# Embedding moved out of its own stage into the first layer, and a third up slice in front of the projection

## Chip, cores and metric

One core of a Trainium2 chip runs the whole program. The metric is device time in microseconds; the median of the runs before is 5509.81 us (three runs, 5508.85 to 5511.06).

## The reference

32 sequences of 256 tokens, hidden width 192, 12 heads of 16. The part that the change touches:

```python
h = layer_norm(emb_word[input_ids] + emb_pos[:S][None], emb_ln_s, emb_ln_b)
for l in range(L):                       # L = 4, banded attention (+-64 tokens)
    a = band_attention(heads(h@Wq+bq), heads(h@Wk+bk), heads(h@Wv+bv), mask)
    h = layer_norm(h + a @ Wo[l] + bo[l], ln1_s[l], ln1_b[l])
    f = gelu(h @ W1[l] + b1[l])          # exact GELU, 4 x 192 columns
    h = layer_norm(h + f @ W2[l] + b2[l], ln2_s[l], ln2_b[l])
```

Behind it come `h + attn(layernorm(h))`, causal with rotary positions, and `h + moe(layernorm(h))`, 16 experts that choose their tokens, with a shared expert.

## The kernel before

`build` calls three stages, each in blocks of its own: `embed`, `tower` and `route`.

**embed** (lines 210 to 352) works on tiles of 128 tokens x 192. SyncE loads ids, positions, norm weights and the mask. VectorE cleans the ids (L295 to L299) and widens the mask by a maximum over 129 neighbours (L301 to L314); SyncE stores that mask to `am_d`. GpSimd gathers rows of the word table with one indirect transfer per tile (L273), 64 in all, and takes the root's power (L281). VectorE adds positions (L323), takes moments (L325, L328, L330) and normalises (L336, L343), four tiles at a time; SyncE writes them to `hbuf` in HBM (L258), which holds the hidden state of every layer.

**tower** starts with constants (loads from L1288, the columns of the mask from `am_d` at L1295) and `setup_dve`, whose casts and fills end in the semaphore `c_ok` (9), on which TensorE and GpSimd wait. Then `token_layers` runs the four layers, and a causal layer follows in the next block. Sequences go in pairs, one in slot 0 and one in slot 1. A **half-turn** works on five sequences at once, one per role, and every engine has its own in-order list for it (`tensor_token`, `scalar_token`, `vector_token`, `pool_token`, and `half` on SyncE):
- G: transpose the hidden state, project to queries and keys, split them into bf16 parts in `stack`.
- V: values; SyncE transposes the stack into `qkT` (L1324); the row maxima (L982) stand at the end of VectorE's list.
- F: first scores, whose row maxima are subtracted later.
- K: second scores, exponentials, products, the sums and the division on VectorE (L1008 to L1020), attention transposed (L453, ScalarE's copy `hT` in L776), projection (L580), residual and norm (L1050 to L916), transposed again (L589).
- B: the MLP of the sequence before: up (`pe_up`, L618 and L621), GELU (L815), down (`pe_down`, L632), residual sum (L1071) and norm.

Layer 1 begins with four half-turns in which only G, then G and V, and so on have work. Each layer is a loop of 14 pairs of half-turns and four written out. `pe_up` makes its six slices of 128 columns in two steps: `UP_BEGIN` in front of the projection, `UP_REST` behind it:

```python
            if K:
                pe_att_T(ph, pe, K)
            if B:
                pe_up(ph, pe, B, G, F, UP_BEGIN)
            if K:
                pe_project(ph, pe, K)
            if B:
                pe_up(ph, pe, B, G, F, UP_REST)
```

SyncE's half-turn issues, in this order: residual (F), transposes (V), hidden state of the next pair (G), maxima's transpose and copy (F), masks (F), a weight load, store (B). It waits in order for each.

Of the kernel before, what the change touches and what calls it, by code (L numbers as in the profile page):

```python
# [65 lines left out]
SCORE_LINKS = 1  # L66


NPAIR = 3
UP_BEGIN = (0, 1)  # L70
UP_REST = (2, 3, 4, 5)
# [119 lines left out]
def build(nc, a, out, B, L, V):  # L191
    ctx = ExitStack()
    with ctx:
# [10 lines left out]
        embed(nc, a, hbuf, am_d, B, V, (L + 1) * N)  # L204
        tower(nc, a, hbuf, am_d, xs, sd, out, B, L)
# [4 lines left out]
def embed(nc, a, hbuf, am_d, B, V, HROWS):  # L210

    N = B * S
    NT = N // P
    G = 4
    STEPS = NT // G
    PAST = 2
    MASK_LINKS = 15
    with ExitStack() as ctx:
        sb = lambda name, shape, dt: ctx.enter_context(nc.sbuf_tensor("emb_" + name, shape, dt))
        sem = Semaphores(nc)  # L220
        ids_raw = sb("ids_raw", [P, NT], I32)
        idf = sb("idf", [P, NT], F32)
        neg = sb("neg", [P, NT], F32)
        ids = sb("ids", [P, NT], I32)
        emb = sb("emb", [P, NT, D], F32)
        pos = sb("pos", [P, T, D], F32)
        lnw = sb("lnw", [P, 2 * D], F32)
        st = [sb(f"st{u}", [P, G, 6], F32) for u in range(2)]
        mv = [sb(f"mv{u}", [P, G, 2], F32) for u in range(2)]
        ve = [sb(f"ve{u}", [P, G], F32) for u in range(2)]  # L230
        half = sb("half", [P, G], F32)
        rstd = [sb(f"rstd{u}", [P, G], F32) for u in range(2)]
        z = [sb(f"z{u}", [P, G, D], F32) for u in range(2)]
        mi = sb("mi", [B, S], I32)
        PADW = S + 2 * W
        mw = [sb("mw0", [B, PADW], F32), sb("mw1", [B, PADW], F32)]
        in_sem, row_sem, mask_sem, am_st = sem("e_in"), sem("e_row"), sem("e_mask"), sem("e_amst")
        ids_ok, gathered = sem("e_ids"), [sem(f"e_gath{g}") for g in range(STEPS)]
        chain, var_ok, rstd_ok, z_ok, z_out, const_ok = (sem("e_chain"), sem("e_var"), sem("e_rstd"), sem("e_z"),
                                                         [sem(f"e_zout{u}") for u in range(2)], sem("e_const"))  # L240
        ctx.callback(sem.close)
        block = ctx.enter_context(nc.Block())

        @block.sync
        def _(sp):
            sp.dma_start(ids_raw[:], a["x"].rearrange("b (t p) -> p (b t)", p=P), allow_slow_non_contiguous=True).then_inc(in_sem, 16)
            sp.dma_start(pos[:], a["emb_pos"].rearrange("(t p) d -> p t d", p=P)).then_inc(row_sem, 16)
            sp.dma_start(lnw[:], a["emb_ln"].to_broadcast([P, 2 * D])).then_inc(row_sem, 16)
            sp.dma_start(mi[:], a["mask"]).then_inc(mask_sem, 16)

            sp.wait_ge(chain, MASK_LINKS)
            for c, f0, w in BAND_COLS:
                sp.dma_start(am_d[0:B, c:c + w], mw[0][:, f0:f0 + w]).then_inc(am_st, 16)
                sp.dma_start(am_d[B:B + NST, c:c + w], mw[0][0:NST, f0:f0 + w]).then_inc(am_st, 16)
            for g in range(STEPS):
                sp.wait_ge(z_ok, g + 1)
                rows = hbuf[g * G * P:(g + 1) * G * P, :]
                sp.dma_start(rows.rearrange("(t p) d -> p t d", p=P), z[g % 2][:]).then_inc(z_out[g % 2], 16)  # L258
                if g == 0:
                    rows = hbuf[HROWS:HROWS + G * P, :]  # L260
# [23 lines left out]
        def _(dve):  # L284
# [63 lines left out]
            for g in range(STEPS):  # L348
                if g + 1 < STEPS:
                    moments(g + 1)  # L350
# [1677 lines left out]
```

## Time and profile before

| | |
|---|---|
| median of the runs | 5509.81 us |
| the profiled execution | 5544.22 us, span 5542.4 us |
| TensorE busy | 5064.9 us (91%), 41842 matmuls |
| VectorE busy | 3498.0 us (63%) |
| ScalarE busy | 2573.6 us (46%) |
| GpSimd busy | 1152.9 us (21%) |
| mean granted TensorE clock | 0.978 of full |

A row of the instructions in time gives the start in us from the span's start, the time it took (merged with its like if there is a count xN), engine, source line, operation, what it writes and reads, and in brackets the idle time of the engine before it with what ended it. PEld is TensorE's weight load, SPq a transfer's issue on SyncE's queue. The table by stretches gives, for a stretch and its length, busy us and count of TensorE, its weight loads, VectorE, ScalarE and GpSimd, then the granted clock, the DMA engines' share and GB/s. "issue" is idle time for which the profile shows no releaser. Matmuls are pipelined; their starts say more than their ends.

### The profile page before, as it was taken

How to read it: one execution, taken by the hardware profiler on the slowest of the kernel's cores; microseconds unless marked ns; L12 is line 12 of the kernel's file. 1: busy time of each engine (PE TensorE's matmuls, PEld its weight loads, DVE VectorE, ACT ScalarE, POOL GpSimd, SP SyncE). 2: the span in 40 equal slices, each digit the busy share in tenths (PEclk: the TensorE clock that was granted, in tenths of full speed). 3: DMA queues.
4: the chain of work that ended last, by engine and by line, in shares of the span. 5: the costliest groups of instructions: out<-in, count | busy, mean ns of one | idle time of the engine just before them, and what ended most of it. 6: DMA issues, size and time to landing. Idle time of an engine off the chain costs nothing. (4 is left out here: it accounts for less than half of the span.)

```text
span 5542.4 us, 119208 instructions
## 1 busy us (share of the span) xinstructions
PE 5064.9 (91%) x41842; PEld 3972.4 (72%) x41842; DVE 3498.0 (63%) x8963; ACT 2573.6 (46%) x5128; POOL 1152.9 (21%) x1048
## 2 busy tenths in 40 slices
PE   0799999999999999999999999969999954999999
PEld 0577777777777777777777777747777742777766
DVE  6566666666666666666666666567777745333332
ACT  0355555555555555555555555535555630111111
POOL 6111111111111111111111111100000001545453
PEclk9999999999999999999999999989999976999999
DMA  6544444444444444444544444344444420333232
GB/s 106 105 88 92 97 92 89 107 93 98 91 88 90 103 101 95 89 88 94 105 101 88 90 97 94 67 93 96 92 101 95 95 69 17 65 83 81 67 87 41
DMA packets 1283995, 488.94 MB, mean 88 GB/s; under 512 B 1086659, under 2 KB 1270560, under 8 KB 1283872
## 3 DMA queue, kind: packets, MB, share of 16 engines
q1 hardware_dynamic: 1256224, 450.63, 37.3%
q0 software_dynamic: 27648, 36.72, 4.3%
q8 instruction: 71, 1.16, 0.1%
q14 instruction: 52, 0.43, 0.0%
HBM read 162.82 MB, written 60.28 MB: 40 GB/s over the span
## 5 line engine op out<-in xcount | busy, mean ns | idle before, releaser
L764 ACT ACTIVATE pT<-banks 128x384 f32<-128x384 f32 x1920 | 924.9, 491 | 768.8 <-PE banks L533 758.1
L982 DVE TENSOR_REDUCE mx<-banks 128x4 f32<-128x768 f32 x768 | 719.4, 950 | 294.3 <-PE banks L514 294.3
L1165 POOL TENSOR_TENSOR rstd<-ve,half 128x2 f32<-128x2 f32 x288 | 218.8, 760 | 3062.4 <-DVE ve L891 3062.4
L496 PE MATMUL banks<-maskb,eyeb 128*128 128x384 bf16 (+1 forms) x2304 | 719.0, 312 | 91.6 <-DVE mx L986 27.0
L514 PE MATMUL banks<-qkT 128*128 128x192 bf16 (+2 forms) x3840 | 633.5, 247 | 0.0
L533 PE MATMUL banks<-qkT 128*128 128x192 bf16 (+2 forms) x3840 | 630.8, 247 | 0.0
L632 PE MATMUL banks<-w,pT 128*128 128x192 f32 x3072 | 554.5, 330 | 0.0
L632 PEld LDWEIGHTS banks<-w,pT 128*128 128x128 f32 x3072 | 492.7, 190 | 42.4 <-issue 21.9
L496 PE MATMUL banks<-mseq,eyeb 128*128 128x384 bf16 x1536 | 501.9, 327 | 9.1 <-issue 4.4
L618 PE MATMUL banks<-nT,w 128*128 128x256 f32 x1920 | 472.5, 382 | 6.6 <-DMA b<-in_b 3.1
L1910 PE MATMUL ps_g<-exp_xT,exp_wg 64*128 64x512 f32 x1152 | 466.8, 600 | 10.8 <-issue 5.4
L1910 PE MATMUL ps_u<-exp_xT,exp_wu 64*128 64x512 f32 x1152 | 456.8, 592 | 4.8 <-DMA emb_emb<-in_emb_word,emb_ids 4.6
L533 PEld LDWEIGHTS banks<-qkT 128*128 128x128 bf16 x3840 | 376.8, 98 | 114.9 <-issue 0.9
L514 PEld LDWEIGHTS banks<-qkT 128*128 128x128 bf16 x3840 | 377.9, 98 | 106.9 <-issue 2.4
L474 PE MATMUL banks<-wqk,hTa 97*128 97x384 f32 (+1 forms) x1280 | 448.7, 492 | 4.3 <-ACT hTa L772 2.7
L815 ACT ACTIVATE pT<-banks,b 128x256 f32<-128x256 f32 x768 | 294.4, 483 | 336.7 <-PE banks L621 336.7
L554 PE MATMUL banks<-pT,vaug 128*32 128x192 f32 (+3 forms) x10752 | 413.5, 284 | 2.5 <-ACT pT L764 1.3
L1690 ACT ACTIVATE exp_sg<-ps_g 128x512 f32<-128x512 f32 x192 | 114.6, 597 | 643.9 <-PE ps_g L1910 558.9
L795 ACT ACT_TABLE_LOAD x320 | 410.6, 1283 | 5.7
L1807 DVE TENSOR_TENSOR exp_hid<-exp_sg,ps_u 128x512 f32<-128x512 f32 x192 | 132.1, 688 | 424.1 <-PE ps_u L1910 361.5
L618 PEld LDWEIGHTS banks<-nT,w 128*128 128x128 f32 x1920 | 347.3, 191 | 42.0 <-DMA b<-in_b 3.6
L554 PEld LDWEIGHTS banks<-pT,vaug 128*32 128x32 f32 x10752 | 284.5, 109 | 121.4 <-ACT pT L764 48.0
(202 smaller groups left out, 8745.1 us busy)
## 6 DMA issues: line engine op xcount, KB each, us to landing
hcur<-hbuf SPq DMA_DIRECT2D x164, 192.0 KB
resid<-hbuf SPq DMA_DIRECT2D x160, 192.0 KB, 2.5
amb<-am_d SPq DMA_DIRECT2D x130, 192.0 KB, 3.0
hbuf<-hout SPq DMA_DIRECT2D x128, 192.0 KB, 2.0
exp_wg<-in_ewg SPq DMA_DIRECT2D x16, 768.0 KB
exp_wu<-in_ewu SPq DMA_DIRECT2D x16, 768.0 KB
exp_wd<-in_ewd SPq DMA_DIRECT2D x16, 576.0 KB
xs<-xr SPq DMA_DIRECT2D x32, 272.0 KB, 2.2
```

The lines of the kernel that those rows point to most:

```text
L474: last = nc.tensor.matmul(bank[s][1 + t][:, 0:2 * D], hTa[s][rows_of(c), c, t * P:(t + 1) * P], wqk[rows_of(c), c, :], start=(c == 0), sto ...
L496: nc.tensor.matmul(part(dst), eyeb[:], part(mask), start=True, stop=ph is not tok)
L514: last = nc.tensor.matmul(dst[:, c0:c0 + w], qT[s][:, h, t * P:(t + 1) * P], kT[s][:, h, f0:f0 + w], start=False, stop=(t == T - 1), skip_ ...
L533: last = nc.tensor.matmul(dst[:, c0:c0 + w], kT[s][:, h, t * P:(t + 1) * P], qT[s][:, h, f0:f0 + w], start=False, stop=(t == T - 1), skip_ ...
L554: last = nc.tensor.matmul(dst[32 * j:32 * j + 32, at + f0:at + f0 + w], vaug[s][:, t, 4 * g + j, :], pT[s][:, (4 * g + j) % NPT, c0:c0 + w ...
L618: nc.tensor.matmul(up_bank(s, f), w1[:, f % 2, up_cols(ph, f)], nT[s][:, f % 2, :], start=True, stop=False)
L632: last = nc.tensor.matmul(bank[1 - s][0][:, t * D:(t + 1) * D], flat_pT(s)[:, f * S + t * P:f * S + (t + 1) * P], w2[:, f, :], start=(f == ...
L764: ph.inc(nc.scalar.activation(pT[s][:, h % NPT, :], bank[s][h % 2][:, 0:SCOLS], ACT.Exp, scale=SCALE), "p", s)
L795: ph.inc(nc.scalar.activation(spare[B.s][:, k:k + 1], zero[:], func), "tb", B.s)
L815: ph.inc(nc.scalar.activation(flat_pT(s)[:, f * S:(f + 1) * S], up_bank(s, f), ACT.Gelu, bias=b1[:, f:f + 1]), "g", s)
L982: last = nc.vector.tensor_reduce(mx[s][:, :, at].rearrange("p t h -> p h t"), src[:, :, 0:SCOLS].rearrange("p h (t k) -> p h t k", t=T), A ...
L1910: last = nc.tensor.matmul(dst[k % 2][:], w[u][rows, c, f * P:(f + 1) * P], xT[rows, c, n0:n0 + HALF], start=start, stop=stop)
```

## The change

`embed` goes, with its block and its end. `tower` loads ids, mask, positions and norm weights first; `first_dve` cleans the ids and widens the mask as before and makes the fills that were in `setup_dve`. GpSimd gathers the first two pairs. VectorE embeds sequences (0, 0) and (1, 0) straight into `hcur` (the numbers are slot and pair), runs the rest of `setup_dve`, then embeds (0, 1) and (1, 1) into two buffers `ring`. SyncE writes all four to `hbuf`. The other 28 are embedded one per half-turn in the first layer, two pairs ahead (argument `X`): GpSimd takes the root and later gathers the next sequence, once the ring buffer's old content has landed in `hbuf`; VectorE takes the moments at the head of its list and normalises in front of the projection's sum; SyncE stores the rows behind the mask load. Without a K (the first three half-turns) VectorE does both parts behind the stack. `load_hidden` waits until the rows are in `hbuf`. The first layer is a loop of its own on GpSimd, VectorE and SyncE. `UP_BEGIN` has three slices instead of two, in all layers and in the causal one.

```diff
+EMBED_AHEAD = 2
-UP_BEGIN = (0, 1)
-UP_REST = (2, 3, 4, 5)
+UP_BEGIN = (0, 1, 2)
+UP_REST = (3, 4, 5)
...
+        def embed_moments(dve, X):
+            s, x, ch = X.s, embed_rows(X), Chain(em, dve, X, "el")
+            dve.wait_ge(*((first_in[s], 16 * T) if x is hcur[s] else (gathered[s], X.it * (16 * T))))
+            ch.inc(nc.vector.tensor_tensor(x[:], x[:], pos[:], ALU.add))
+            ch.wait()
+            for t in range(T):
+                last = nc.vector.bn_stats(est[s][:, t, :], x[:, t, :])
+            ch.inc(last)
+            ch.wait_apart(row_in, 32)
+            for t in range(T):
+                last = nc.vector.bn_aggr(emv[s][:, t, :], est[s][:, t, :])
+            ch.inc(last)
+            ch.wait()
+            em.inc(nc.vector.tensor_scalar(eve[s][:], emv[s][:, :, 1], 1e-12, None, ALU.add), "var", s)
+            return ch
+
+        def embed_normalise(dve, X, ch):
+            s, x = X.s, embed_rows(X)
+            for t in range(T):
+                last = nc.vector.scalar_tensor_tensor(x[:, t, :], x[:, t, :], emv[s][:, t, 0:1], lnw[:, 0:D],
+                                                      ALU.subtract, ALU.mult)
+            ch.inc(last)
+            em.wait(dve, "rstd", s, X.it)
+            ch.wait()
+            for t in range(T):
+                last = nc.vector.scalar_tensor_tensor(x[:, t, :], x[:, t, :], erstd[s][:, t:t + 1], lnw[:, D:2 * D],
+                                                      ALU.mult, ALU.add)
...
+        def vector_token(ph, dve, G, V, F, K, B, X=None):
+            if X and K:
+                ec = embed_moments(dve, X)
             if K:
                 s = K.s
                 bc = Chain(ph, dve, K, "bl")
...
             if G:
                 dve_rest(ph, dve, G)
+            if X and K:
+                embed_normalise(dve, X, ec)
             if K:
                 ph.wait(dve, "wo_ps", s, K.it)
...
                 dve_stack(ph, dve, G, bass.ds(G.pair * (NST * T) + G.s * T, T))
+            if X and not K:
+                embed_normalise(dve, X, embed_moments(dve, X))
...
+        def pool_gather(pool, X):
+            s = X.s
+            early = isinstance(X.it, int) and X.it < EMBED_AHEAD
+            at = ids[:, X.it * (NST * T) + s * T:(X.it + 1) * (NST * T)] if early else now[s]
+            if not early:
+                pool.wait_ge(z_out[s], X.it * 16 + 16)
+                nc.gpsimd.tensor_copy(now[s][:], ids[:, bass.ds(X.it * (NST * T) + s * T, T)]).then_inc(now_ok[s], 1)
+                wait_apart(pool, now_ok[s], X.it - 1, ids_ok, 1)
+            for t in range(T):
+                pool.indirect_dma_start(embed_rows(X)[:, t, :], None, a["emb_word"],
+                                        bass.IndirectOffsetOnAxis(ap=at[:, t:t + 1], axis=0)
+                                        ).then_inc((first_in if embed_rows(X) is hcur[s] else gathered)[s], 16)
...
+        def pool_token(ph, pool, G, V, F, K, B, X=None):
             if F:
                 pool_masks(ph, pool, F)
+            if X:
+                pool_embed_rstd(pool, X)
             if K:
...
+            if X:
+                pool_gather(pool, embed_turn(1 - X.s, X.it + X.s))
             if B:
                 pool_rstd(ph, pool, B, "var2", "rstd2")
...
+                def store_rows(X):
+                    s = X.s
+                    wait_apart(sp, z_ok[s], X.it, c_in, 112)
+                    rows = hbuf[bass.ds(X.it * (NST * S) + s * S, S), :]
+                    sp.dma_start(rows.rearrange("(t p) d -> p t d", p=P), ring[s][:]).then_inc(z_out[s], 16)
+                def load_hidden(G, embedded):
                     tok.wait_apart(sp, "hT_ps", G.s, G.it, None, c_in, 112)
+                    if embedded:
+                        wait_apart(sp, z_out[G.s], G.it * 16 + 48, c_in, 112)
                     load_h(G.it + 1, G.s)
...
                     if F:
                         sp_maxima(tok, sp, F, c_in, 112)
                         load_masks(F)
+                    if X:
+                        store_rows(X)
                     if load:
                         load()
                     if B:
                         store(B)
...
                 load_qk(0)
+                load_v(0)
+                set_up()
                 for s in ST:
-                    load_h(0, s)
                     load_am(0, s)
-                load_v(0)
+                for s in ST:
+                    first_rows(s)
+                for s in ST:
+                    store_rows(embed_turn(s, 1))
                 load_back(0)
                 load_ffn(0)
...
             def _(dve):
-                setup_dve(dve)
-                token_layers(dve, vector_token)
+                first_dve(dve)
+                for it in range(2):
+                    ec = [embed_moments(dve, embed_turn(s, it)) for s in ST]
+                    for s in ST:
+                        embed_normalise(dve, embed_turn(s, it), ec[s])
+                    if it == 0:
+                        setup_dve(dve)
+                token_layers(dve, vector_token, True)
```

`set_up` waits for the widened mask, stores it to `am_d`, waits until it has landed and loads the columns back. `first_rows` writes `hcur` of a slot to `hbuf` twice (layer rows and the spare rows at the end, as `embed` did). `pool_embed_rstd` is the root's power, `embed_rows` names the buffer, `embed_turn` a turn without weights.

## Rows read from the trace of the kernel before

**Rows 1.** Table by stretches, layer 1: stretch, us, busy (count) per engine.
```profile
480.00:906.00 426.00, 423.77 (x3757) 338.90 (x3757) 293.89 (x760) 241.15 (x480) 77.80 (x81) 1.00 0.45 93
```

**Rows 2.** Instructions in time, embedding stage; last row: DMA issues, to landing.
```profile
9.13 1.16 POOL L273 DMA_INDIRECT emb_emb<-in_emb_word,emb_ids  x1 [8.27 <-DVE emb_ids L299]
...
15.69 0.35 DVE L314 TENSOR_SCALAR emb_mw<-emb_mw 32x256 f32<-32x256 f32 x1
...
emb_emb<-in_emb_word,emb_ids POOLq DMA_INDIRECT x64, 4.1
```

**Rows 3.** Instructions in time, set-up to first scores and row maxima.
```profile
130.65 9.38 SPq L1295 DMA_DIRECT2D amc<-am_d  x2
...
144.39 0.23 DVE L1256 CAST eyeb<-eye 128x128 bf16<-128x128 f32 x1 [20.75 <-DMA amc<-am_d]
...
146.05 0.70 DVE L1268 MEMSET vaug<- 128x768 f32 x1
...
152.46 0.06 DVE L1282 MEMSET rstd<- 128x2 f32 x1
...
158.58 1.06 PE L453 MATMUL banks<-eye,hcur 128*96 128x128 f32 x4 [158.58 <-DMA hcur<-hbuf]
...
169.73 0.22 DVE L973 CAST stack<-kb 128x24 bf16<-128x24 f32 x1
...
184.85 0.50 PE L496 MATMUL banks<-maskb,eyeb 128*128 128x384 bf16 x1 [14.14 <-DMA qkT<-stack]
...
200.71 1.82 DVE L982 TENSOR_REDUCE mx<-banks 128x4 f32<-128x768 f32 x2
```

**Rows 4.** Line 1324, stack transposes: ns of an issue; us to landing.
```profile
L1324 SPq DMA_TRANSPOSE qkT<-stack x256: 3582/3894/9104, 170.0 to 3533.8; - x128
...
DMA to landing us min/median/max: 5.5/5.9/8.9
```

**Rows 5.** Instructions in time, a steady half-turn: TensorE, then VectorE.
```profile
657.88 1.47 PE L486 MATMUL banks<-wv,hTa 97*128 97x192 f32 x8
...
659.19 0.82 PE L565 MATMUL banks<-eye,oT 128*128 128x128 f32 x6
...
662.87 1.03 PE L618 MATMUL banks<-nT,w 128*128 128x256 f32 x4
...
663.91 1.57 PE L580 MATMUL banks<-wo,hT 97*128 97x192 f32 x8
...
665.32 1.89 PE L618 MATMUL banks<-nT,w 128*128 128x256 f32 x8
...
670.69 0.27 PE L589 MATMUL banks<-eye,h 128*128 128x128 f32 x1
...
660.19 0.37 DVE L1008 TENSOR_SCALAR den<-banks,amp 128x12 f32<-128x12 f32 x2 [2.36 <-PE banks L565]
...
663.47 0.62 DVE L925 SCALAR_TENSOR_TENSOR rem<-banks,live,stack 128x384 f32<-128x384 f32 x1 [0.64 <-ACT stack L748]
...
665.62 0.56 DVE L1050 TENSOR_TENSOR h<-banks,resid 128x384 f32<-128x384 f32 x1 [1.54 <-PE banks L580]
...
667.22 0.17 DVE L891 TENSOR_SCALAR ve<-mv 128x2 f32<-128x2 f32 x1
...
668.45 0.75 DVE L916 SCALAR_TENSOR_TENSOR h<-h,rstd,vec 128x192 f32<-128x192 f32 x2 [0.36 <-POOL rstd L1165]
```

**Rows 6.** Groups by line, 160:3600, then causal: busy, mean, idle before.
```profile
L580 PEld LDWEIGHTS banks<-wo,hT 97*128 97x128 f32 (+1 forms) x1024 | 165.4, 191 | 45.2 <-ACT hT L776 26.5 <-issue 18.4
...
L580 PEld LDWEIGHTS banks<-wo,hT 97*128 97x128 f32 (+1 forms) x256 | 41.8, 192 | 7.3 <-ACT hT L776 7.1
```

**Rows 7.** Instructions in time, last stage: indirect transfers beside VectorE.
```profile
4784.77 0.74 DVE L1778 TENSOR_SCALAR sel_oh_lo<-sel_oh_lo,sel_partc 128x2048 bf16<-128x2048 bf16 x1
...
4784.90 2.05 POOL L1661 DMA_INDIRECT out<-exp_yb,exp_idx  x1 [0.30 <-DVE exp_yb L1816]
...
4787.25 1.56 POOL L1661 DMA_INDIRECT out<-exp_yb,exp_idx  x1 [0.30 <-issue]
```

More of the change, by code:

```diff
@@ L425, in tower @@
         zero = sb("zero", [P, 1], F32)
+        ids_raw = sb("ids_raw", [P, NT], I32)
+        idf = sb("idf", [P, NT], F32)
+        neg = sb("neg", [P, NT], F32)
+        ids = sb("ids", [P, NT + T], I32)
+        pos = sb("pos", [P, T, D], F32)
+        lnw = sb("lnw", [P, 2 * D], F32)
+        est = sbs("est", [P, T, 6], F32)
+        emv = sbs("emv", [P, T, 2], F32)
+        eve = sbs("eve", [P, T], F32)
+        erstd = sbs("erstd", [P, T], F32)
+        ring = sbs("ring", [P, T, D], F32)
+        now = sbs("now", [P, T], I32)
+        PADW = S + 2 * W
+        mi = sb("mi", [B, S], I32)
+        mw = [sb("mw0", [B, PADW], F32), sb("mw1", [B, PADW], F32)]
         spare = sbs("spare", [P, 2], F32)
@@ L1228, in token_layer, with layer_end @@
+            layer_end(eng, half_of, l, last)
+        def layer_end(eng, half_of, l, last):
             n, it = PAIRS - 2, l * PAIRS + (PAIRS - 2)
@@ L1351, in load_ffn, with half @@
                     sp.dma_start(b1[:], a["b1"][bass.ds(l, 1)].rearrange("o p n -> (o p) n")).then_inc(w_ffn, 16)
-                def half(G, V, F, K, B, load=None):
+                def half(G, V, F, K, B, load=None, embedded=False, X=None):
                     if F:
@@ L1367, in half, with layer, two @@
                         store(B)
-                def layer(l, last):
-                    def two(i, load=None):
+                X = lambda s, it: embed_turn(s, it + EMBED_AHEAD)
+                def layer(l, last, embeds=False):
+                    def two(i, load=None, embedded=False, embed=False):
                         it = l * PAIRS + i
                         half(turn(0, it + 2, i + 2, l), turn(1, it + 1, i + 1, l), turn(0, it + 1, i + 1, l),
-                             turn(1, it, i, l), turn(0, it, i, l))
+                             turn(1, it, i, l), turn(0, it, i, l), None, embedded, X(0, it + 2) if embed else None)
                         half(turn(1, it + 2, i + 2, l), turn(0, it + 2, i + 2, l), turn(1, it + 1, i + 1, l),
-                             turn(0, it + 1, i + 1, l), turn(1, it, i, l), load)
+                             turn(0, it + 1, i + 1, l), turn(1, it, i, l), load, embedded, X(1, it + 2) if embed else None)
                     n, it = PAIRS - 2, l * PAIRS + (PAIRS - 2)
@@ L1389, in next_back @@
                         load_back(l + 1)
-                    with sp.Fori(0, PAIRS - 3) as i:
-                        two(i)
+                    if embeds:
+                        with sp.Fori(0, PAIRS - 2 - EMBED_AHEAD) as i:
+                            two(i, None, True, True)
+                        for i in range(PAIRS - 2 - EMBED_AHEAD, PAIRS - 3):
+                            two(i, None, True)
+                    else:
+                        with sp.Fori(0, PAIRS - 3) as i:
+                            two(i)
                     two(PAIRS - 3, next_qk)
```

284 lines of the change are left out of this document (118 added, 166 removed).

## Prediction

> **What bounds the kernel now.** I read the table by stretches first, then the order of instructions at the start and in one steady half-turn, then what the weight loads waited for. Where the layers run, TensorE is busy 423.77 us of 426 while VectorE is at 69% [rows 1]. So the time is the length of TensorE's stream, plus the stretches in which it has nothing. The largest of these is the start: TensorE's first instruction, a transposition, stands at 158.58 us, and the first scores at 184.85, after 14.14 us of waiting for a transposing transfer [rows 3]. Nothing of the first layer needs more than four embedded sequences, so most of this wait is order, not work. A second, small hole comes back in every half-turn: the projection waits for ScalarE's copy of the transposed attention. Over the four layers the weight loads of L580 stood idle 45.2 us before 128 projections, 0.35 us each [rows 6].
>
> **The sum is made against the profiled execution**, 5544.2 us, span 5542.4. The median of the runs is 34.4 us lower; I take the difference of the two kernels from the profile and put it on the median, 5509.8.
>
> **Part 1, the embedding stage goes.** I follow the new order to the first scores.
> - VectorE starts alike: indices ready at about 9.1, when the first gather starts, and the mask chain ends at 16.0 [rows 2]. Then the fills that stood at 146.05 to 152.5 [rows 3]: 6.5 us, to 22.5.
> - Four gathers for two sequences take 4 x (1.16 + 0.3) from 9.1 and land about 4.1 later [rows 2], so before 22.5: no wait. One sequence is 384 columns wide; add, moments and aggregate have the form of the chain from L1050 to L891, 665.62 to 667.39, so 1.8 us. Its four scale-and-shift instructions take 0.75 a pair like L916 [rows 5], with their links 1.6. Two sequences: 6.8 us, to 29.3.
> - The set-up waits for the column loads of the mask. Their issue began at 130.65 and they were in at 144.39, 14 us later, behind another element-wise load of the same number of elements, so half of it is theirs [rows 3]; alone I take 8. SyncE stores the mask at 16 to 17.5, waits until it has landed (about 20) and loads it: 28.5, hidden by VectorE's 29.3. By the old 14 it is 34: the late end, 5 us. The set-up itself is 1.6 us (144.39 to 146.05): 30.9. TensorE starts at about 31.5.
> - VectorE then embeds the next two, to 37.7. The first stack needs 11.3 us from TensorE's start (158.58 to 169.9 [rows 3]): 42.8, not delayed by it.
> - **What is late next** is the queue. SyncE's first half-turn now ends with the store of sequence (0, 2), in front of the transposes of the first stack. That store waits for VectorE, which waits for the gather, which waits until the store of (0, 1) has landed. Store at 36, landed 38.5, GpSimd's copy and two gathers to 41.2, landing 45.3, and up to 2 more beside the weights of the back half, whose loads are issued at that time: 47. VectorE takes 1.8 + 0.8 + 1.6: 51. The transposes start at 51.5 instead of 43 and are in place 3.9 (the issue of one) + 5.9 (its landing) [rows 4] later: first scores at about 61.5 instead of 184.85, **123 us earlier**.
> - The pipe's filling has one more price. In the third half-turn the embedding of (0, 3), 3.4 us, stands on VectorE between the stack and the row maxima, which began at 200.71 right behind the stack [rows 3]. TensorE may run four heads ahead, no more: **3 us lost**. Net **-120**. Early end (everything at its row, no loss in filling): -126. Late end (column loads 5 later, gathers delayed 4 by the weights, 2 more in filling): -109.
>
> **Part 2, one sequence per half-turn in layer 1.** 28 of them. Added per half-turn: on VectorE 3.4 us, on GpSimd 0.8 for the root and about 3 for a copy and two gathers, on SyncE's queue one 192 KB store. TensorE gets nothing. VectorE runs its list in order, so the two places count. The moments stand in front of the attention sums: VectorE is free there from 657.83 and waits 2.36 us for TensorE until 660.19 [rows 5]; 1.8 us fit, 0.5 is left. The normalising stands in front of L1050: VectorE is free from 664.09 and waits 1.54 us for the projection until 665.62 [rows 5]; 1.6 us end at 665.7, and the projection itself will be 0.1 later (part 3). Who waits for it is the transposition of the result at 670.69 [rows 5], and the norm ends at 669.2: 1.4 us to spare. The gathers are issued some 10 us before their data are read. The store stands in SyncE's queue behind the mask load and in front of the store of the hidden state, where the queue waits for VectorE anyway. I take **+1 us** in all; bounds 0 and 28 x 0.5 = 14, if both cover pieces are missed.
> A GpSimd instruction can also get into VectorE's way. In the last stage an indirect transfer that began 0.13 us behind an in-SBUF VectorE operation took 2.05 us, against 1.56 for the next, and the VectorE operation kept its 0.74 us [rows 7]. So GpSimd pays, and it has the time. The Trainium skill, "SBUF — State Buffer", Who interferes with whom, says that whichever of the two starts first holds the shared port pair for the whole instruction and the other fully blocks. By that rule a gather that starts first would stop the copies of the stack, which the rows here don't show; it is rival B.
>
> **Part 3, the third slice in front of the projection.** Eight matmuls of 192 columns keep a pitch of (659.19 - 657.88) / 8 = 0.164 us where nothing is awaited, so four of 256 columns take 0.87. L618 begins at 662.87 and should be through at 663.74; L580 begins at 663.91 and takes 1.41 to the next instead of 1.31 [rows 5]. The hole is 0.17 + 0.10 = 0.27 us; the idle weight load (0.35) is the upper end, 0.17 the lower. One slice of 0.44 us put there fills it, since the copy it waits for is over by then: TensorE's stream gets shorter by 0.27, while the projection ends 0.1 later against the rest, covered by the 1.4 us above. The slice's bank held the attention sums that VectorE has read before the transposition in front of L618, so it brings no wait. 127 half-turns: **-34** (bounds -22 and -45, and zero, rival A). In the causal layer the idle weight load is 7.3 us over 32 projections, 0.23 each [rows 6], and other waits on VectorE follow: I take -1, bounds 0 and -7. The two-layer loops and the block boundary that goes cost nothing further: the boundary lies within the 158 us already counted.
>
> Sum: -120 + 1 - 34 - 1 = **-154**. 5509.8 - 154 = **5356 us**; the profiled execution would be 5390.
>
> **Rivals.**
> A. The hole at the projection only moves: the slice taken from behind the projection was covering the wait for GELU or for the result, and TensorE stands there instead. For it: TensorE's down products follow ScalarE's GELU closely, and GELU follows the up slices. Against it: both hang on the end of the up slices, and move with them. Gain of part 3 zero: 5391 us. Chance 0.17.
> B. VectorE or the port is late in the first layer: the copies of the stack, then the residual sum, then the first scores each lose about 1 us per half-turn, 28 x 1: 5384. For it: the first scores wait for the residual sum, which follows the stack closely. Against it: VectorE's operation kept its time in [rows 7]. Chance 0.15.
> C. Slower than before: the new ring closes on itself. Gather, moments, normalising, store, landing and the next gather into the same buffer form a chain that must fit into two half-turns, about 53 us (the 128 of four layers lie between 160 and 3600 us [rows 6], 26.9 each with filling and draining). Its links are 3 + 4.1 + 4.2 + a wait in SyncE's queue + 2.5. If SyncE's in-order queue put more than a half-turn between its steps, each sequence would cost up to 26 us more and the 28 up to 364, half of them for both buffers: 5356 + 182 = 5538. It decides only from 5.5 us per half-turn on, where the 154 are used up. The links sum to 14 us and leave 39 free, so chance 0.03.
> The change failing to start earlier (a wait for the old stage's whole output kept somewhere) is not in the diff; the only such wait is for rows of the next pair. It is inside the late end.
>
> **How the numbers follow.** Forecast 0.65, A 0.17, B 0.15, C 0.03. With the ends of part 1 (-126, -109), part 2 (0, +14) and part 3 (-45, -22) the forecast's own range is 5335 to 5385, as the ends rarely meet; A and B reach 5391, with a late start 5400. Range 5332 to 5400. A difference under 0.2% (11 us) can't be told from none: faster 0.96, same 0.01, slower 0.03.
>
> **What would show it.** TensorE's first instruction near 31 and the first scores near 62; if the scores come at 53, the queue argument is wrong, if past 72, the column loads or gathers are. In the third and fourth half-turns a TensorE wait for a row maximum of about 3 us. In layer 1 a half-turn as long as in layer 2: longer by 1 means B, and then the stack's copies are longer or the waits of L1008 and L1050 are gone with TensorE idle. In all layers no idle weight load in front of L580 and 0.27 us less per half-turn; if L580's wait is gone and the half-turn is as long as before, A holds. I am wrong if the first layer's half-turns grow by several us, or if the start gains under 109.

## The result, and the profile after

| | before | after |
|---|---|---|
| median of the runs, us | 5510.44 | 5384.03 |
| lowest to highest | 5508.85 to 5511.4 | 5379.45 to 5388.73 |
| profiled execution, span | 5542.4 | 5386.9 |
| TensorE's first instruction | 158.58 | 54.79 |
| first scores | 184.85 | 86.02 |
| first hidden state stored (L1335, after: L1352) | 259.13 | 164.49 |
| last hidden state stored | 3604.9 | 3486.55 |
| last stage begins (`sel_gt`, L1727, after: L1775) | 4608.6 | 4487.3 |

The ratio is 0.9771 [0.9754, 0.9788]: 126.4 us faster, where 154 were forecast; 5384 lies in the range of 5332 to 5400. The two profiled executions are 155.5 us apart, but 34 of these lie behind `sel_gt`, where the change does nothing, and go with the chip, as the runs below show. Up to `sel_gt` the difference is 121.3 us, and that is what I explain. It has four parts, each read from two rows of the table: up to the first scores 98.8; from there to the first store the kernel after is 4.2 slower (78.5 against 74.3); between the first and the last store it is 23.7 faster; behind it 2.9 faster. One plainly slow execution, the 12069 us of e8 below, is left out of every median here.

TensorE is as full as before. This is the table by stretches of the kernel after, over the stretch of [rows 1]: stretch, us, busy (count) of TensorE, its weight loads, VectorE, ScalarE, GpSimd, then granted clock, DMA share, GB/s.

```profile
480.00:906.00 426.00, 423.99 (x3799) 343.40 (x3788) 326.59 (x873) 243.38 (x486) 111.44 (x124) 1.00 0.51 106
```

It stands in layer 1, where the embedding now runs: VectorE went from 69% to 77% (326.59 / 426) and GpSimd from 18% to 26%, and TensorE stayed as busy as in [rows 1].

The start is where the forecast failed. Instructions in time of the kernel after, first SyncE's queue, then VectorE, then TensorE (start, us, queue or engine and line, operation, idle before):

```profile
10.80 0.58 SPq L1287 DMA_DIRECT2D kb_i<-in_mask  x1
11.43 9.70 SPq L1355 DMA_DIRECT2D wqk<-in_wqkv  x1
21.17 10.44 SPq L1358 DMA_DIRECT2D wv<-in_wqkv  x1
31.66 9.63 SPq L1292 DMA_DIRECT2D am_d<-mw  x1
...
46.18 2.92 SPq L1297 DMA_DIRECT2D amc<-am_d  x2
...
75.31 0.39 SPq L1318 DMA_DIRECT2D hbuf<-ring  x1
75.81 8.30 SPq L1341 DMA_TRANSPOSE qkT<-stack  x2
...
53.18 0.23 DVE L1263 CAST eyeb<-eye 128x128 bf16<-128x128 f32 x1 [23.80 <-DMA amc<-am_d]
...
71.79 0.56 DVE L920 TENSOR_TENSOR ring<-ring,pos 128x384 f32<-128x384 f32 x1 [5.49 <-DMA ring<-in_emb_word,now]
...
54.79 1.09 PE L330 MATMUL banks<-eye,hcur 128*96 128x128 f32 x4 [54.79 <-DVE kb L1273]
...
86.02 0.50 PE L373 MATMUL banks<-maskb,eyeb 128*128 128x384 bf16 x1 [19.43 <-DMA qkT<-stack]
```

VectorE embedded the first two sequences between 22.5 and 29.4, within 0.1 us of the forecast, and then stood idle 23.80 us for `amc`. The mask's store (`am_d`) could have gone out at 16 (in e1 below it does, at 15.88), but in SyncE's queue two issues stand in front of it, `wqk` with 9.70 and `wv` with 10.44 us, and its own first issue took 9.63. The rates show what these were doing. The view of the DMA traffic of the same kernel over 0 to 60 us, one figure for each 1.5 us (busy share in tenths, then GB/s):

```profile
DMA  0069978889999997420000000001100297979920
GB/s 0 0 5 7 7 34 208 134 285 339 151 74 56 68 63 57 53 56 25 26 26 25 26 25 26 24 23 39 39 24 4 2 7 5 8 99 287 324 76 0
```

From 27 to 40.5 us the mean share of the 16 DMA engines is under a tenth, and they move 25 GB/s. Over this stretch the table by stretches gives a share of 0.07, and 0.07 x 16 is about one: a single engine is draining something, and the queue waits behind it.

One steady half-turn of layer 1 in the kernel after, to be read beside [rows 5]; TensorE, VectorE, GpSimd (the last row from an earlier half-turn):

```profile
643.39 1.46 PE L495 MATMUL banks<-nT,w 128*128 128x256 f32 x6
644.69 1.47 PE L457 MATMUL banks<-wo,hT 97*128 97x192 f32 x8
646.00 1.46 PE L495 MATMUL banks<-nT,w 128*128 128x256 f32 x6
...
640.69 0.38 DVE L885 TENSOR_SCALAR den<-banks,amp 128x12 f32<-128x12 f32 x2 [0.67 <-PE banks L442]
...
645.37 0.75 DVE L942 SCALAR_TENSOR_TENSOR ring<-ring,erstd,lnw 128x192 f32<-128x192 f32 x2
646.30 0.56 DVE L969 TENSOR_TENSOR h<-banks,resid 128x384 f32<-128x384 f32 x1 [0.19 <-PE banks L457]
...
258.72 1.06 POOL L1109 DMA_INDIRECT ring<-in_emb_word,now  x1 [0.80 <-POOL now L1106]
```

Three slices (six matmuls) now stand on each side of the projection, and the projection (L457) takes 1.31 us to the next instead of 1.41. Both embedding pieces fit where the forecast put them: VectorE still waits 0.67 us for the attention sums (2.36 before) and 0.19 us for the projection (1.54 before). The groups by line, 160 to 3600 us, show that the hole of [rows 6] is nearly closed, 45.2 us idle before, 7.6 after:

```profile
L457 PEld LDWEIGHTS banks<-wo,hT 97*128 97x128 f32 (+1 forms) x1024 | 175.0, 190 | 7.6 <-ACT hT L653 0.9
```

### The profile page after: what moved, and what is told of

Same layout as the page of the kernel before. It is cut to its first block and busy times, and to the rows that moved or that the text cites. A ratio compares the mean times of both kernels' runs of the same rounds, so it can differ in the third digit from the quotient of the medians.

```text
span 5386.9 us, 119439 instructions
## 1 busy us (share of the span) xinstructions
PE 5019.4 (93%) x41842; PEld 3994.9 (74%) x41842; DVE 3503.2 (65%) x8996; ACT 2570.7 (48%) x5128; POOL 1158.5 (22%) x1094
## 5 line engine op out<-in xcount | busy, mean ns | idle before, releaser
L1958 PE MATMUL ps_u<-exp_xT,exp_wu 64*128 64x512 f32 x1152 | 470.8, 589 | 0.0
```

The source lines that it names most:

```text
L1958: last = nc.tensor.matmul(dst[k % 2][:], w[u][rows, c, f * P:(f + 1) * P], xT[rows, c, n0:n0 + HALF], start=start, stop=stop)
```

## The experiments

Every kernel here computes everything. The experiments ran on three chips, the second to fourth of the table; which chip the first result came from is not on record. Each kernel is compared with the kernel before on its own chip, and absolute times of different chips are not compared. "Pitch" is the mean distance of two stores of a hidden state in mid-layer.

| kernel | chip | median | against before there | first scores | pitch, layer 1 / 2 and 3 / 4 | last stage begins |
|---|---|---|---|---|---|---|
| before | first | 5510.44 | | 184.85 | 26.484 / 26.484 / 26.44 | 4608.6 |
| after | first | 5384.03 | -126.4 | 86.02 | 26.235 / 26.242 / 26.234 | 4487.3 |
| e1_weights_behind | second | 5418.25 | -125.3 | 80.43 | | 4481.3 |
| e2_split_weights | second | 5397.53 | -146.0 | 68.08 | | 4461.4 |
| e3_two_slices | second | 5446.96 | -96.6 | 82.93 | 26.478 / 26.485 / 26.443 | 4507.6 |
| e5_only_slices | third | 5508.17 | -27.2 | 182.55 | 26.241 in all | 4574.8 |
| e6_after_again | third | 5414.41 | -120.9 | 81.33 | as after | 4482.0 |
| e7_split_kb_early | third | 5396.14 | -139.2 | 67.51 | as after | 4460.7 |
| e8_transposes_first | third | 5394.55 | -140.8 | 66.00 | as after | 4467.1 |
| e9_split_layers | fourth | 5368.21 | -142.3 | 67.93 | as after | 4462.6 |
| e10_layer0_again | fourth | 5366.71 | -143.8 | 68.43 | as after | 4467.5 |

### e1_weights_behind: the mask ahead of the weights

```
-                load_qk(0)
-                load_v(0)
                 set_up()
+                load_qk(0)
+                load_v(0)
```

> The changed kernel with the loads of wqk and wv moved behind the mask's store and column loads. Theory: the set-up came at 53.2 instead of 29 us because these two loads (97 partitions, they drain at 25 GB/s with about one of 16 DMA engines busy) fill the queue in front of the mask's store, whose issue ran from 31.7 to 41.3. Then the mask's store is issued at 16 to 18, the columns are in by 30 to 37 (kb_i's elements, in until 26.8, still lie in front), the set-up moves from 53.2 to 30-37; but wqk then lands only near 45, and the first projection waits for it instead: first scores 8 to 14 us earlier than 86.0, time 5370 to 5376. Rival (the element-wise loads of ids and kb_i alone clog the queue, the weights don't matter): the mask's store is still issued past 30, time unchanged at 5384.

0.9774 [0.9758, 0.979] of before, no better than the kernel after. The set-up came in the expected stretch (34.20), but the first scores came only 2.5 us earlier than in e3 on the same chip (80.43 against 82.93), where 8 to 14 were expected. The trace, SyncE's queue and TensorE:

```profile
15.88 7.39 SPq L1292 DMA_DIRECT2D am_d<-mw  x1
...
26.95 2.95 SPq L1297 DMA_DIRECT2D amc<-am_d  x2
29.94 2.73 SPq L1355 DMA_DIRECT2D wqk<-in_wqkv  x1
32.71 7.12 SPq L1358 DMA_DIRECT2D wv<-in_wqkv  x1
...
35.82 1.09 PE L330 MATMUL banks<-eye,hcur 128*96 128x128 f32 x4 [35.82 <-DVE kb L1273]
...
47.08 5.46 PE L351 MATMUL banks<-wqk,hTa 97*128 97x384 f32 x8 [10.17 <-DMA wqk<-in_wqkv]
```

TensorE started 19 us earlier (35.82 instead of 54.79) and then waited 10.17 us for Wq. What looked like an order of two things in a queue is a length: both weights and the mask are needed before anything can go on, and the weights are slow. Two smaller facts: even without the weights in front, the mask's first issue took 7.39 us, behind `kb_i`; and `amc` was in 7.25 us after its issue (VectorE's set-up began at 34.20), for which the forecast took 8.

### e2_split_weights: the same bytes, 96 rows and 1 row

Wq|Wk and Wv of the first layer are tiles of 97 partitions (96 and the bias). Here each is loaded as 96 and 1.

```
+                def split(dst, c0, c1, done):
+                    for r0, r1, sem_ in ((0, DC, done), (DC, DC + 1, w_one)):
+                        sp.dma_start(dst[r0:r1], a["wqkv"][0:1, r0:r1, :, c0:c1]...).then_inc(sem_, 16)
...
-                load_qk(0)
-                load_v(0)
+                split(wqk, 0, 2 * D, w_qk)
+                split(wv, 2 * D, 3 * D, w_v)
                 set_up()
...
                 pe.wait_ge(c_ok, 9)
+                pe.wait_ge(w_one, 32)
```

> The changed kernel with the first loads of wqk and wv each cut into 96 partitions and the one bias partition, same place in the queue. Theory that the 97-partition form runs on one DMA engine: the 96 spread over all, no stretch at 25 GB/s is left, wqk and wv are through about 2 us behind kb_i, the mask's store is in by 28-30, the set-up starts at 35-38 instead of 53.2, first scores 15 to 18 us earlier, time 5366 to 5370. Rival (the number of elements or bytes in the queue blocks it, whatever the partitions): store's issue past 35 as before, time 5384.

0.9741 [0.9725, 0.9757]. SyncE's queue, VectorE, TensorE, and the DMA rates over 0 to 60 us:

```profile
10.68 0.56 SPq L1288 DMA_DIRECT2D kb_i<-in_mask  x1
11.28 11.42 SPq L1360 DMA_DIRECT2D wqk<-in_wqkv  x2
22.75 1.28 SPq L1360 DMA_DIRECT2D wv<-in_wqkv  x2
24.07 0.39 SPq L1293 DMA_DIRECT2D am_d<-mw  x1
...
28.46 2.98 SPq L1298 DMA_DIRECT2D amc<-am_d  x2
...
35.34 0.23 DVE L1264 CAST eyeb<-eye 128x128 bf16<-128x128 f32 x1 [5.87 <-DMA amc<-am_d]
...
68.08 0.50 PE L374 MATMUL banks<-maskb,eyeb 128*128 128x384 bf16 x1 [18.78 <-DMA qkT<-stack]
...
GB/s 0 0 4 7 7 36 190 134 313 342 132 83 61 78 57 60 135 244 41 1 6 6 7 126 309 317 37 0 129 131 122 192 366 331 315 196 41 27 52 171
```

The plateau at 25 GB/s is gone (135 and 244 in its place), `wv`'s issue fell from 10.44 to 1.28 and the mask's from 9.63 to 0.39. The first scores come at 68.08: 18 us before the kernel after, 13 to 15 before the two other kernels whose start is that of after (e6 81.33, e3 82.93). The gain against before is 146.0 us, 20 more than after. This is most of the forecast's miss at the start: the partition count of a load, not its bytes. The Trainium skill, "DMA: Bandwidth & Descriptors", section on why a DMA increments its semaphore by 16, gives the rule: the number of DMA engines is the largest one up to 16 that divides the slowest dimension of both sides, so 96 partitions use 16 and 97, a prime, use one. The trace agrees: 25 GB/s at under a tenth of the engines with 97, 135 and 244 GB/s with 96.

It is not all of it. `wqk`'s own issue did not get shorter (11.42 us for its two parts, most of it the first). What it waits behind is `kb_i`, the load of 8192 single elements: in e7 below `kb_i` stands elsewhere, and `wqk`'s two parts are issued in 1.50 us. And the set-up starts at 35.34, still 6 us behind the 29.3 of the forecast.

### e3_two_slices and e5_only_slices: each half of the change alone

```
-UP_BEGIN = (0, 1, 2)
-UP_REST = (3, 4, 5)
+UP_BEGIN = (0, 1)
+UP_REST = (2, 3, 4, 5)
```

e3 is the kernel after with this edit, e5 the kernel before with its reverse.

> The changed kernel with two slices in front of the projection, as before the change. Theory: all of the shorter half-turn comes from the third slice, nothing from the embedding: half-turns of 26.48 us instead of 26.24 in every layer, 127 x 0.243 = 31 us, less some 7 that were lost at layer ends anyway and plus up to 4 in the causal layer: 5408 to 5415. Rival (part of the saving comes from leaving out the embedding stage, or embedding costs something that the third slice hid in layer 1): layers 2 to 4 at 26.48 but layer 1 above it by 0.2 to 0.5, time 5415 to 5425.

> The kernel before with nothing but the third slice in front of the projection. Theory (third slice alone shortens the half-turn from 26.484 to 26.241; at each of the three layer ends 5 to 6 us come back, because the next layer's weights are waited for whatever the pace; causal layer -4): 127 x 0.243 = 31, less 5 to 10, plus 4: 24 to 29 us faster than before. Rival (the slices and the embedding need each other, or the third slice brings its full 31 plus 4 once the start is the old one): 33 to 36 us faster.

e3: 0.9829 [0.9813, 0.9845], pitch 26.48 again, in layer 1 as in layers 2 and 3: the whole gain in pitch is the slice's, and the embedding of one sequence per half-turn costs nothing that shows (the pitch of layer 1 is within 0.01 us of that of layer 2). e5: 0.9952 [0.9936, 0.9969], 27.2 us faster than before, pitch 26.241. The two halves add up: 96.6 + 27.2 = 123.8, beside 126.4 and 120.9 measured for both. Rival A (nothing from the slice) would have needed e5 at 0 and falls; so does B (1 us per half-turn of layer 1), as the pitches of the layers differ by under 0.01 us.

### e4_before_again and e6_after_again: is the last stage shorter?

The profile of the kernel after ran 899.6 us from `sel_gt` to its end, that of before 933.8, and nothing there was changed.

> The kernel before, once more. The profiled executions differ by 155.5 us, the medians by 126.4; 34 of the difference lie behind 4608 us, in the expert stage, where the change touches nothing. Theory: that is the execution, not the change: a second profile of the kernel before has an expert stage of about 900 us (4608.6 to the end) instead of 934 and a span near 5510. Rival (the expert stage really gained): it is 934 again.

> The changed kernel itself, for the comparisons of this chip. The expert stage took 34 us longer on the chip of the first four runs, for the kernel before too, so absolute times can't be carried over. Expected here: 119 to 127 us faster than before, set-up at 53, first scores at 86 us, as in its first profile.

e4 took 5546.0 us (one execution) and its last stage again 935 us, so the expectation that a second profile would show 900 failed. e6 took 5414.4 (0.9783 [0.9767, 0.9799] of before) with 927. e7 and e10 are one program: 933 us on the third chip, 900 on the fourth. So it goes with the chip: where before takes 5510 us the last stage takes 900 to 903 (after, e9, e10), where it takes 5535 to 5544 the stage takes 927 to 936 (e1 to e8). The profile of the kernel before, 5544.2 us with a last stage of 933.8, looks like one of the second kind, though the median shown with it is of the first; the record does not name its chip. Table by stretches, 300 us in the last stage, of e4 and of e10:

```profile
5109.00:5409.00 300.00, 294.19 (x1746) 212.22 (x1745) 108.86 (x156) 50.90 (x83) 145.68 (x93) 1.00 0.34 81
```
```profile
4968.00:5268.00 300.00, 298.99 (x1884) 228.77 (x1882) 111.05 (x166) 50.18 (x82) 145.97 (x92) 1.00 0.33 77
```

At the same granted clock e10 gets 1884 matmuls into 300 us and e4 1746, with TensorE idle 1.0 against 5.8 us. Why the same stage runs thinner there on some chips stays open. It touches the change nowhere: both kernels' gain is the same on either kind of chip (-126.4 and -120.9, intervals overlapping).

### e7_split_kb_early and e8_transposes_first: what holds the rest of the start

e7 is e2 with the 8192-element load of the mask's columns (`kb_i`) issued behind `mi` instead of behind the constants. e8 adds the order that my forecast named as late: the first stack's transposes ahead of the store of sequence (0, 2).

```
                 sp.dma_start(mi[:], a["mask"]).then_inc(mask_in, 16)
+                sp.dma_start(kb_i[:], ...)
...
                 sp.dma_start(rope[:], a["c_rope"]).then_inc(c_in, 16)
-                sp.dma_start(kb_i[:], ...)
...
-                half(turn(0, 0, 0, 0), None, None, None, None, None, True, X(0, 0))
-                half(turn(1, 0, 0, 0), turn(0, 0, 0, 0), None, None, None, None, True, X(1, 0))
+                half(turn(0, 0, 0, 0), None, None, None, None, None, True)
+                transposes(turn(0, 0, 0, 0), None)
+                load_hidden(turn(1, 0, 0, 0), True)
+                store_rows(X(0, 0))
+                store_rows(X(1, 0))
```

> e2 (wqk and wv of the first layer cut in 96 partitions and 1) with the element-wise load kb_i moved in front, behind the ids and the mask. Theory: what was left of the delay in e2 is kb_i's 8192 elements, queued ahead of the mask's store; in front they are through before the mask is widened. Set-up at 29 to 31 us instead of 35.3 in e2, first scores at 61 to 64 instead of 68.1: the start as I predicted it, 4 to 7 us faster than e2, about 24 faster than the changed kernel. Rival (the column loads alone take the time, or gathers and ids are delayed by kb_i as much): set-up stays at 35, or the indices come 5 us later; no gain over e2.

> e7 with SyncE's store of the sequence (0, 2) moved behind the first two transposes. Theory A (my prediction: the transposes wait for the store, so the queue order costs): the transposes start 9 us earlier, right behind the stack, first scores 5 to 9 us earlier, and the whole as much. Theory B (VectorE's list is as late: it embeds (1, 2), whose gather lands last, before the first row maximum): the first scores come earlier, but the first row maximum starts within 2 us of where it did, about 19 us behind the stack; total gain 0 to 2 us.

e7: 0.9752 [0.9736, 0.9768], 18.3 us below e6 on the same chip, and no execution of the one reaches into those of the other (5394.7 to 5403.3 against 5411.1 to 5417.3). This is the cleanest price of the split, with the move of `kb_i` in it, which is worth little (first scores 67.51 against 68.08 in e2). The early load only moved its own price: `pos` behind it now took 5.03 us to issue. The mask's store went out at 19.25 instead of 24.07, but took 6.2 us from its last issue to the load of `amc` where e2 took 2.9, so `amc` went out at 27.68 (28.46 in e2) and the set-up began at 34.66, not at 29 to 31. SyncE's queue, with VectorE's set-up:

```profile
7.48 0.42 SPq L1282 DMA_DIRECT2D kb_i<-in_mask  x1
7.95 5.03 SPq L1283 DMA_DIRECT2D pos<-in_emb_pos  x1
...
16.30 1.50 SPq L1360 DMA_DIRECT2D wqk<-in_wqkv  x2
...
19.25 0.60 SPq L1293 DMA_DIRECT2D am_d<-mw  x1
...
27.68 2.91 SPq L1298 DMA_DIRECT2D amc<-am_d  x2
...
34.66 0.23 DVE L1264 CAST eyeb<-eye 128x128 bf16<-128x128 f32 x1 [5.09 <-DMA amc<-am_d]
```

e8: 0.9744 [0.9724, 0.9763], the same as e7. The transposes did go out ten microseconds earlier, but the first scores came only 1.5 us earlier, as the second theory had it. SyncE, VectorE, TensorE of e8:

```profile
47.46 14.75 SPq L1342 DMA_TRANSPOSE qkT<-stack  x2
62.94 6.26 SPq L1319 DMA_DIRECT2D hbuf<-ring  x2
...
65.28 0.56 DVE L921 TENSOR_TENSOR ring<-ring,pos 128x384 f32<-128x384 f32 x1 [4.38 <-DMA ring<-in_emb_word,now]
68.66 5.58 DVE L860 TENSOR_REDUCE mx<-banks 128x4 f32<-128x768 f32 x6
...
84.10 0.50 PE L374 MATMUL banks<-mseq,eyeb 128*128 128x384 bf16 x1 [6.14 <-DMA qkT<-mrT]
```

Two things took the gain. The pair of transposes is now issued right behind the weights of the back half (43.3 to 46.5) and takes 14.75 us to issue instead of 8.25. And the stores that were moved behind them delay the next gather, for which VectorE waits 4.38 us with the row maxima behind it in its list. The next scores came at 84.10, in e7 at 82.69. The queue held the start, but with that order gone, the gathers and VectorE are as late.

### e9_split_layers and e10_layer0_again: the ends of the layers

The kernel after loses 5.1 to 6.9 us over its pitch where one layer ends and the next begins. e9 splits the weight loads of all four layers as e2 did the first; e10 is e7 once more.

```
+                def rows_apart(dst, src, l, c0, c1, done):
+                    for r0, r1 in ((0, DC), (DC, DC + 1)):
+                        sp.dma_start(dst[r0:r1], src[bass.ds(l, 1), r0:r1, :, c0:c1]...).then_inc(done, 16)
...
-                    sp.dma_start(wo[:], a["wo"][bass.ds(l, 1)]...).then_inc(w_back, 16)
+                    rows_apart(wo, a["wo"], l, 0, D, w_back)
```

> The weight loads of all four layers (Wq|Wk, Wv, Wo) are split into 96 rows and 1 row; in e7 only those of the first layer are. The rest is e7 (early load of the mask's columns). Theory A (what the layer ends cost is the weights' loads: 97 partitions go through one of 16 DMA engines, and the small transposes of row maxima that share it come late): each of the three layer ends, 5 to 7 us above the pitch in the kernel after, shrinks by 1.5 to 4 us, the transposes of row maxima there take no longer than elsewhere, and the whole is 5 to 12 us below e7. Theory B (what ends late there is the order of TensorE's and VectorE's own work at the end of a layer, no load): the layer ends stay within 0.5 us of e7's each, and the whole within 3 us. Both: the pitch of a half-turn stays 26.24 us, first scores at 67 to 69 us.

> The kernel of e7 once more, on the chip of e9, as its partner. Both theories: pitch 26.24 us, first scores 67 to 69 us, layer ends as in e7; 135 to 142 us below the kernel before if the gain doesn't depend on the chip, while its absolute time may be up to 34 us off e7's with the chip.

0.9743 [0.9727, 0.9759] and 0.9738 [0.9722, 0.9755]: the same. Ten half-turns across each layer end, less ten times the pitch, in us; the last row is how long in all the granted clock stood at its lower level (1.2 GHz, 0.5 in the table by stretches) at these three ends:

| | before | e4 (before) | e3 | after | e6 (after) | e5 | e1 | e2 | e7 | e10 (e7) | e8 | e9 |
|---|---|---|---|---|---|---|---|---|---|---|---|---|
| slices in front | 2 | 2 | 2 | 3 | 3 | 3 | 3 | 3 | 3 | 3 | 3 | 3 |
| layer 1 to 2 | 3.8 | 3.9 | 3.1 | 6.2 | 3.7 | 4.2 | 5.7 | 4.1 | 3.7 | 7.9 | 6.1 | 3.5 |
| 2 to 3 | 7.4 | 6.6 | 4.7 | 6.9 | 5.8 | 4.3 | 7.4 | 6.5 | 6.2 | 5.7 | 6.8 | 5.8 |
| 3 to 4 | 1.5 | 1.5 | 1.1 | 5.1 | 5.3 | 4.9 | 4.0 | 3.3 | 2.0 | 1.8 | 1.4 | 4.8 |
| low clock, us | 6.8 | 3.4 | 0 | 10.2 | 3.4 | 3.4 | 6.8 | 3.4 | 0 | 6.8 | 6.8 | 3.4 |

The theory that the weights' loads are waited for falls: e9 is within the scatter of the others. Much of that scatter has a cause that the traces show. e7 and e10 are one program, and at the first layer end e10 takes 4.2 us more. e9 and e10, the waits of TensorE between 925 and 1000 us (engine, line, releaser: us in total, times, longest), then the table by stretches for 953 to 961 us of e9 and of e10:

```profile
PE banks L373 <- issue: 1.4, 1, 1.4
PE banks L373 <- DMA qkT<-mrT: 1.3, 1, 1.3
```
```profile
PE banks L374 <- issue: 3.1, 1, 3.1
PE banks L374 <- DMA qkT<-mrT: 1.1, 1, 1.1
```
```profile
953.00:961.00 8.00, 8.00 (x123) 6.05 (x121) 7.15 (x15) 4.55 (x10) 2.80 (x3) 1.00 0.04 14
```
```profile
953.00:961.00 8.00, 6.91 (x36) 4.86 (x36) 2.41 (x5) 2.94 (x6) 0.00 (x0) 0.57 0.01 3
```

The transposed maxima cost the same with split and unsplit weights. In e10 the wait with no releaser is 1.7 us longer, and behind this idle of 3.1 us the granted clock fell to half (0.57 over the stretch) for about 7 us; in e9 it stayed at 1.00. The 6.8 us at half the clock cost some 3.4 us, an estimate from the two levels. If half of the last row is taken off the sums, the three kernels with two slices in front of the projection are left with 8.9 to 10.3 us for the three ends, and the nine with three slices with 10.9 to 13.7. So the third slice itself seems to cost about 3 us at the layer ends, which e5 shows too: 27.2 us gained where the pitches alone give 29.7. Where these 3 us are waited for, and what the wait with no releaser is, stays open.

## Why the prediction was right, and where it was not

**The sum of part 1 was mis-sized: -120 forecast, -94.6 measured** at the first store, outside the bounds of -126 and -109 that were given for it. The prediction called itself wrong if the start gained under 109, and by that sign its account of the start was wrong. The time lies in the range because the range reached up to 5400 for rivals A and B; that the miss ended there is luck.

The step that failed is the one on the set-up: "SyncE stores the mask at 16 to 17.5, waits until it has landed (about 20) and loads it: 28.5". Its last part held (a column load takes 7.0 to 7.25 us, I took 8). The rest did not: `am_d` was issued at 31.66 to 42.3 and `amc` only at 46.18. I had counted VectorE's list and not SyncE's: the new order puts the loads of Wq|Wk and Wv between the constants and the mask. TensorE started at 54.79 instead of 31.5, 23.3 late, and from its start to the first scores it took 31.2 us where I had 30: of the miss of 24, 23 are that step. It has two causes. With the weights split (e2) the first scores come 18 us earlier (13 to 15 against e6 and e3), and 146.0 us are gained instead of the 154 forecast. Of what is left, some 6 us lie again in front of the set-up (35.34 against 29.3), where the DMA engines and the queue are still busy with `kb_i` and the constants (in e2 the table by stretches gives them a share of 1.06, that is full, from 18 to 24 us); neither e1 nor e7 got it below 34.20. The stated late end (column loads 5 later) put the delay into the column loads, which were on time, and so did the sign for first scores past 72: it was the store in front of them.

The old trace had the price. In the kernel before, the same loads of 97 partitions are followed by long issues, SyncE's queue, then the table by stretches:

```profile
140.07 2.80 SPq L1338 DMA_DIRECT2D wqk<-in_wqkv  x1
142.91 7.21 SPq L1300 DMA_DIRECT2D hcur<-hbuf  x1
...
152.61 0.66 SPq L1341 DMA_DIRECT2D wv<-in_wqkv  x1
153.31 8.90 SPq L1344 DMA_DIRECT2D wo<-in_wo  x1
```
```profile
156.00:162.00 6.00, 2.75 (x7) 1.73 (x8) 0.00 (x0) 0.58 (x1) 2.75 (x3) 1.00 0.07 24
```

The issue behind `wqk` took 7.21 us, the one behind `wv` 8.90, and the DMA engines moved 24 GB/s at a share of 0.07. The 9.38 us of [rows 3] is the issue behind `kb_i`. The prediction used it for the length of the column loads and not as a sign of what `kb_i` does to a queue.

**The queue as "what is late next" was right as to what waits, wrong as to what it is worth.** The transposes went out 9.5 us behind the finished stack (66.3 to 75.81), where I had 8.5, and behind the store that I named. But e8 takes that order away and gains nothing clear of the scatter: gather, VectorE and the next transfer are as late.

**The loss in filling** was put at 3 us; the first scores to the first store took 4.2 us more than before. It did not show as a wait for a row maximum: TensorE waited 4.01 us for the transposed maxima at 101.40, where before waited 1.62 at 198.31. The next long wait, 3.50 us for the normalised result at 125.95, is no part of the loss: before has it with 3.53. Behind the idle at 101.40 TensorE's granted clock was 0.50 from 100.0 to 106.7, in before 1.00 from 199.0 to 205.7; half of the 5.30 us that TensorE was busy there are 2.6 us, an estimate of what that cost. Right in size, only partly in place, and with a term (the clock) that the forecast did not have.

**Part 2, the embedding per half-turn: +1 forecast, 0 measured** (pitch of layer 1 26.235 against 26.242). Both cover pieces held, with 0.67 us left at the attention sums (I had 0.5) and 0.19 at the projection. The GpSimd gathers, a median of 0.97 us, took no longer than those of the old stage (0.96), and VectorE beside them kept its times (the copies of the stack, L847, 0.246 us each in layer 1 and in layer 2). The Trainium skill's rule on the shared port pair ("SBUF — State Buffer", Who interferes with whom) would have shown as lost time on VectorE in layer 1; no such loss is in these rows.

**Part 3, the third slice: -34 forecast, about -30 in pitch, -27 in the run alone.** 0.27 us per half-turn was forecast from the order of two lines; 0.24 was measured in layers 1 to 3 and 0.21 in layer 4: 96 x 0.243 + 31 x 0.206 = 29.7. The kernel after shows 23.7 between its stores, since the layer ends took 5.5 us more in this pair of executions: 1.7 of them by the lower clock (half of 10.2 - 6.8), the rest most likely by the slice itself, a term that the forecast put at nothing. From the last store to `sel_gt`, where the causal layer lies, 2.9 us were gained (1 forecast, 7 the bound), but none in e6 (1004.2 us against the 1003.7 of before).

In all: -98.8 + 4.2 - 23.7 - 2.9 = -121.2 (121.3 before rounding), where the forecast had -123 + 3 - 33 - 1 = -154. Of the 33 missing, 24 lie before the first scores, nearly all of them in the one step on the set-up, and 9 in the layers. The time came out where rivals A and B had put theirs (5391 and 5384), but by neither's mechanism: e3 and e5 exclude both. Without the pitch of layer 1, 5384 would have read as a proof of B. Of rival C nothing shows; its price was also unclear in itself, since 28 sequences at 26 us shared by two buffers are 364, which the prediction halved once more to 182.

## What to carry to other kernels

- When a stage that hid the start goes, write down every queue from time zero, the loads too that had been free. What a load costs that nobody waited for is in the old trace, as the issue time of the row behind it (7.21 and 8.90 us here) and as a stretch of low DMA share.
- Look at the partition count of each load that becomes urgent. An odd row for a bias (97) put the tile on one DMA engine here and held up what was issued behind it; loading 96 and 1 brought the first scores forward by 13 to 18 us and the end by 18 (e7, which also moves `kb_i`, against e6), and the two more issues cost nothing that shows. The best kernel of the study is the changed one with that edit (0.974 of before, against 0.977; the intervals touch, the executions of e6 and e7 on one chip do not).
- A gain in the steady state can be read to a tenth of a microsecond from the gap between two lines; what comes out at the end has a few microseconds per layer end on top, part of it from falls of the granted clock, so measure the pitch and look at the clock, and not only at the time.

## What the chip showed that I had not expected

- A load of 97 partitions (291 KB and 145.5 KB) moved 25 GB/s at a share of 0.07, about one of 16 DMA engines, and the next issues in the same queue took 9.63 and 10.44 us (7.21 and 8.90 in before); as 96 and 1 the later ones took 0.39 to 1.28.
- A load of 8192 single elements (`kb_i`, 32 KB) took 16.0 us to land in the kernel after, and the issue behind it took 5.03 us (e7, `pos`), 7.39 (e1, the mask's store), 9.70 (after, `wqk`) or 9.38 (before, `amc`, both issues).
- The start of one program scatters: TensorE's first instruction came at 54.79 in the kernel after and at 50.61 in e6, with `wqk` and `wv` at 9.70 + 10.44 and at 8.00 + 8.42 us.
- The last stage, untouched, takes 900 to 903 us on one kind of chip (the fourth, and that of the first result) and 927 to 936 on two others, at the same granted clock of 1.00 in the stretch shown.
- At a layer end an idle of 3.1 us of TensorE was followed by about 7 us at half the granted clock (e10), an idle of 1.4 us by none (e9).
